# A graph attention edge loop in which VectorE adds the gathered rows to half of the scores

## The reference

```
s     = x_l[src] + x_r[dst] + e_attr @ W_e.T      # one row of 4 x 64 per edge
s     = leaky_relu(s, 0.2)
alpha = einsum('ehc,hc->eh', s, att)              # one score per edge and head
ex    = exp(alpha - segment_max(alpha, dst)[dst])
alpha = ex / (segment_sum(ex, dst)[dst] + 1e-16)
out   = segment_sum(alpha[..., None] * x_l[src], dst) + bias
```

## Time and profile before

| what | value |
|---|---|
| median of the runs | 3526.07 us |
| the profiled execution | 3518.4 us |
| its span | 3516.8 us |
| TensorE (PE) busy over the span | 3182.1 us, 90% |
| VectorE (DVE) | 1879.7 us, 53% |
| ScalarE (ACT) | 1363.2 us, 39% |
| GpSimd (POOL) | 1247.5 us, 35% |
| score products, line 1311, first and last start | 148.2 and 1376.5 us |

### The profile page before, as it was taken

The page is one execution under the profiler, slowest core; times in us unless marked ns, Lnnn a source line. Parts: engine busy times, 40 slices in busy tenths (PEclk is TensorE's granted clock), DMA queues, the critical chain, the costliest instruction groups (busy, mean ns, idle before and its releaser), DMA issues. The chain is left out here.

```text
span 3516.8 us, 52606 instructions
## 1 busy us (share of the span) xinstructions
PE 3182.1 (90%) x14467; PEld 2583.5 (73%) x14468; DVE 1879.7 (53%) x3767; ACT 1363.2 (39%) x4647; POOL 1247.5 (35%) x1195
## 2 busy tenths in 40 slices
PE   2799999999999999378998899799989896999998
PEld 1677777777777776266777677677867695888887
DVE  5677878777787787873436444633634330111102
ACT  0047677677777767431223113122312121222222
POOL 2376666666666663132103100300200043001016
PEclk9899999999999999588999999899989888999999
DMA  4576766766677665341111010000000143333323
GB/s 135 160 187 166 168 167 166 165 166 166 162 169 172 170 166 98 111 157 30 30 40 30 8 36 26 8 1 14 26 37 1 45 126 97 125 117 120 121 83 109
DMA packets 302415, 358.71 MB, mean 102 GB/s; under 512 B 164807, under 2 KB 223772, under 8 KB 298314
## 3 DMA queue, kind: packets, MB, share of 16 engines
q0 software_dynamic: 68240, 181.29, 19.9%
q1 hardware_dynamic: 233510, 173.64, 18.5%
q10 hardware_dynamic: 560, 2.35, 0.2%
HBM read 299.08 MB, written 57.01 MB: 101 GB/s over the span
## 5 line engine op out<-in xcount | busy, mean ns | idle before, releaser
L1311 PE MATMUL a_pS<-g_xr,a_lt 128*128 x1680 | 522.1, 393 | 26.1 <-DMA XS<-xl_d,a_ix 20.6
L1294 POOL DMA_INDIRECT a_g<-xl_d,a_ix x480 | 461.6, 962 | 220.9 <-PE a_pS L1312 133.2
L1405 ACT ACTIVATE b_m<-a_g,c_pcx 128x64 f32<-128x64 f32 x1856 | 454.6, 333 | 0.0
L1319 PE MATMUL b_pM<-b_m,b_oh 128*112 128x281 f32 x1680 | 443.6, 403 | 5.1 <-DVE g_acc L1447 3.5
L1440 DVE SCALAR_TENSOR_TENSOR a_r<-a_pS,g_attx 128x528 f32<-128x528 f32 x420 | 296.8, 707 | 242.5 <-PE a_pS L1312 233.6
L1294 POOL DMA_INDIRECT XS<-xl_d,a_ix x360 | 345.2, 959 | 134.9 <-issue 89.2
L113 POOL TENSOR_TENSOR m_rstd<-m_ve,m_mhalf 125x5 f32<-125x5 f32 x45 | 53.0, 1178 | 928.5 <-DVE m_ve L103 920.0
L1311 PEld LDWEIGHTS a_pS<-g_xr,a_lt 128*128 128x128 f32 x1680 | 310.6, 191 | 87.4 <-issue 30.0
L1319 PEld LDWEIGHTS b_pM<-b_m,b_oh 128*112 128x112 f32 x1680 | 291.0, 176 | 101.4 <-issue 10.7
L1994 ACT ACTIVATE f_hid<-f_pH,f_b 128x256 f32<-128x256 f32 (+2 forms) x360 | 169.2, 470 | 486.0 <-PE f_pH L1906 485.5
L421 PE MATMUL m_pH<-m_h,m_w 128*128 128x312 f32 (+1 forms) x1280 | 341.9, 428 | 7.7 <-DVE m_h L566 7.7
(11 more groups left out here) (348 smaller groups left out, 4444.7 us busy)
## 6 DMA issues: line engine op xcount, KB each, us to landing
a_db<-dl_d SPq DMA_DIRECT2D x212, 224.0 KB
f_w<-in_ffn_W1p SPq DMA_DIRECT2D x32, 1024.0 KB
m_w<-in_mix_W SPq DMA_DIRECT2D x8, 1024.0 KB
xg_d<-m_zero POOLq DMA_DIRECT2D x1, 8192.0 KB, 33.1
f_w<-in_ffn_W2p SPq DMA_DIRECT2D x8, 1024.0 KB
f_xg<-xg_d POOLq DMA_DIRECT2D x32, 256.0 KB, 3.7
y_d<-f_y POOLq DMA_DIRECT2D x32, 256.0 KB, 3.2
a_g<-xl_d,a_ix POOLq DMA_INDIRECT x480, 5.6
```

The source lines that it names most:

```text
L1294: p.indirect_dma_start(out=gathered(t)[:, j, :], out_offset=None, in_=xl_d, in_offset=bass.IndirectOffsetOnAxis(ap=IX[:, t // BSTEPS, n:n ...
L1311: pe.matmul(o, lt[:, j, :], XRW[:, bass.ds(ws[h], 1), :].rearrange("p a d -> p (a d)"), start=True, stop=False)
L1319: ins = pe.matmul(pM[0:WN, h, 0:MW], OH[:, b, j, :], M[:, b, j, :], start=(j == 2 * h), stop=(j == 2 * h + 1))
L1405: ins = a.activation(m[:, j, part], gathered(ts)[:, j, part], ACT.Copy, scale=of[:, first + j, h, 0:1])
```

## The change

`LIFTED` names five of the seven steps of a batch, tau 2 to 6. In these steps the identity product of the second pair is left out on TensorE. VectorE adds the gathered rows to the second pair instead (`lift`, from PSUM and SBUF into `a_r`), and gates that in place later, behind the one-hot for the sums (`lifted_gate`, from SBUF into SBUF). The semaphore that returns the PSUM banks to TensorE is renamed to `a_read0` and `a_read1`; for a lifted pair it is raised by the addition. The reduction of a lifted step also waits for the new gate (`a_gated`). The first pair, and both pairs of tau 0 and 1, are as they were.

```diff
--- before.py
+++ after.py
@@ -54,6 +54,7 @@
 WEIGH, SUM, ADD = 10, 11, 12
 AHEAD = 3
 SLOPE = 0.2
+LIFTED = (2, 3, 4, 5, 6)
 LOW = -float(2 ** 100)
 MH, MD = 8, 32
 FF = 1024
@@ -1305,11 +1306,13 @@
                         lt = LT[:, t % LTS, :, :]
 
                         def scores(h, ws):
-                            wait(pe, f"a_gated{h}", base, t)
+                            lifted = h == 1 and t % BSTEPS in LIFTED
+                            wait(pe, f"a_read{h}", base, t)
                             for j in (2 * h, 2 * h + 1):
                                 o = pS[0:TE, j, 0:GD]
-                                pe.matmul(o, lt[:, j, :], XRW[:, bass.ds(ws[h], 1), :].rearrange("p a d -> p (a d)"), start=True, stop=False)
-                                ins = pe.matmul(o, ident[:, :], gathered(t)[:, j, :], start=False, stop=True)
+                                ins = pe.matmul(o, lt[:, j, :], XRW[:, bass.ds(ws[h], 1), :].rearrange("p a d -> p (a d)"), start=True, stop=lifted)
+                                if not lifted:
+                                    ins = pe.matmul(o, ident[:, :], gathered(t)[:, j, :], start=False, stop=True)
                             ins.then_inc(s[f"a_scored{h}"], 1)
 
                         def sums(h):
@@ -1435,10 +1438,22 @@
                         par = 1 if odd else 0
                         scores = pA[0:CP, 0:TE]
 
+                        lifted = t % BSTEPS in LIFTED
+
+                        def lift():
+                            v.wait_ge(s[f"a_g{t}"], 64 * i + 64)
+                            wait(v, "a_scored1", base, t + 1)
+                            v.tensor_tensor(R[:, 2:4, :], pS[0:TE, 2:4, 0:GD], gathered(t)[:, 2:4, :], ALU.add).then_inc(s["a_read1"], 1)
+
                         def gate(h):
                             wait(v, f"a_scored{h}", base, t + 1)
                             v.scalar_tensor_tensor(out=R[:, 2 * h:2 * h + 2, :], in0=pS[0:TE, 2 * h:2 * h + 2, 0:GD], scalar=0.0,
-                                                   in1=attx[:, :].unsqueeze(1).broadcast_to([TE, 2, GD]), op0=ALU.max, op1=ALU.mult).then_inc(s[f"a_gated{h}"], 1)
+                                                   in1=attx[:, :].unsqueeze(1).broadcast_to([TE, 2, GD]), op0=ALU.max, op1=ALU.mult).then_inc(s[f"a_read{h}"], 1)
+
+                        def lifted_gate():
+                            wait(v, "a_read1", base, t + 1)
+                            v.scalar_tensor_tensor(out=R[:, 2:4, :], in0=R[:, 2:4, :], scalar=0.0,
+                                                   in1=attx[:, :].unsqueeze(1).broadcast_to([TE, 2, GD]), op0=ALU.max, op1=ALU.mult).then_inc(s["a_gated"], 1)
 
                         def add(h, at):
                             wait(v, f"b_summed{h}", base, t - ADD + 1)
@@ -1481,7 +1496,9 @@
                         elif tau == 3:
                             v.wait_ge(s["c_new"], n)
                             v.tensor_tensor(fade[:, :], by_item(ST[0:1, 1 - par, 0, 0:CP])[:, :, BI], pA[0:1, 0:GH], ALU.subtract).then_inc(s["c_step"], 1)
-                        if scoring:
+                        if scoring and lifted:
+                            lift()
+                        elif scoring:
                             gate(1)
                         if weighing and not scoring:
                             ts = (t - WEIGH) % RING
@@ -1495,6 +1512,8 @@
                             wait(v, "b_summed1", base, t - WEIGH - 1)
                             v.tensor_tensor(OH[:, t % 2, :, :], nodes[:, :].unsqueeze(1).broadcast_to([TE, IG, WN]),
                                             DLX[:, four(base, t - WEIGH)].unsqueeze(2).broadcast_to([TE, IG, WN]), ALU.is_equal).then_inc(s["b_onehot"], 1)
+                        if scoring and lifted:
+                            lifted_gate()
                         if tau == 1:
                             v.wait_ge(s["c_cols"], n)
                             v.tensor_copy(IN[:, :], pY[0:CP, 240:242]).then_inc(s["c_init"], 1)
@@ -1509,7 +1528,9 @@
                             v.wait_ge(s["c_step"], n)
                             v.tensor_scalar(fade[:, :], fade[:, :], 0.0, None, ALU.min).then_inc(s["c_less"], 1)
                         if scoring:
-                            wait(v, "a_gated1", base, t + 1)
+                            wait(v, "a_read1", base, t + 1)
+                            if lifted:
+                                v.wait_ge(s["a_gated"], 2 * len(LIFTED) * i + len([k for k in range(t + 1) if k % BSTEPS in LIFTED]))
                             i0 = IG * (t % BSTEPS)
                             v.tensor_reduce(AX_[:, t // BSTEPS, :, i0:i0 + IG].rearrange("p h i -> p i h"), R[:, :, :].rearrange("p i (h d) -> p i h d", h=GH),
                                             AX.X, ALU.add).then_inc(s["a_alpha"], 1)
```

## The result

The changed kernel takes 3496.14 us (median of 4 runs, 3494.87 to 3500.44), the kernel before beside it 3524.1 us. The ratio is 0.9923, 95% interval 0.9905 to 0.994: 28 us faster, where 90 were forecast and 3404 was the low and 3482 the high end. The profiled execution of the changed kernel took 3500.44 us, 18 less than that of before.

The account below looks back on a forecast made before the run. TensorE was taken to bound the edge loop at 41.09 us per batch; 4.45 saved less 1.3 of waiting for VectorE gains 3.15, times 28.6 batches 90 us: 3526 to 3436 us, range 3404 to 3482.

Parts of the forecast that it names:

- TensorE's saving: Edge loop: two identity products fewer per lifted step, 0.89 us, or 4.45 us per batch.
- VectorE's prices: Lifted steps: addition 0.692 us, SBUF gate 0.694, and a self-wait of 0.25; together 0.87 us more per step.
- 37.9 predicted: Edge loop's batch period in us: TensorE's 36.64 plus 1.3 of waiting, against 41.09 before.
- GpSimd's pace when nothing holds it: Edge loop: 1.274 us per gather, so 36.95 us per batch of 29, below the forecast period.
- the 1 us of cover per batch: Edge loop: what GpSimd has left per batch after the change, where before it had 4 us.
- Rival B: Edge loop: gathers become the bound through slipping landing or GpSimd pace; gain 60 to 31 us, 3466 to 3495; 17%.
- rival C: Lifted steps: the new SBUF gate waits for GpSimd's gathers, 0.95 us each; 45 us slower, 3571; 5%.
- a lead of three steps: Gathers ahead of TensorE: 15.6 us, less scores and issuing, so a landing of 8.7 us is still in time.
- TensorE's waits: For VectorE: 0.2 us before the sums of steps 5 and 6, 0.9 before step 0's transpose; 1.3 per batch.

Follow-up runs that it names:

- f1_onehot_first: Changed kernel with the one-hot for the sums moved ahead of the addition in lifted steps; 3448.32 us, ratio 0.9785 to the kernel before.
- f2_extra_gate: Kernel before plus one more VectorE gate in steps 2 to 6, both operands in SBUF, into a scratch buffer; 3524.2 us, ratio 1.0001.
- c2_reduce_for_gate: Changed kernel with the lifted steps' SBUF gate replaced by a reduction of the same columns, one SBUF operand; 3443.22 us, ratio 0.9767 to the kernel before.

## Why the prediction was wrong

**TensorE's saving and VectorE's prices were right.** The passes came at 0.697 and 0.700 for 0.692 and 0.694, and the quicker batches take 37.1 to 37.4 us. In f1_onehot_first, where the gathers are back at 0.962, the period is 38.39. That kernel has one self-wait more than the changed one; with the reduction in the gate's place, which has the changed kernel's order, it is 38.17, for 37.9 predicted. Of the 60 us between 3496 and 3436, these two kernels bring back 53 and 48.

**The step that failed** is "GpSimd's pace when nothing holds it is 17 gathers in 21.66 us, 1.274 each ... 36.95 us", taken over to the changed kernel. The gathers rose by 81.4 us in all. From the first to the last GpSimd now has 888.2 us of gathers, 30 staging gathers of 0.93 (27.9) and 870 gaps of 0.30 (261), 1177 of the 1338.9-142.4 = 1196.5 us: full to 98%, before 1095.7 of 1221.8, 90%. A batch is 29 x (1.057+0.30) = 39.4 us for GpSimd alone, more than TensorE's 36.64 and than my 37.9. GpSimd set the pace on average, and the 1 us of cover per batch that the prediction left it was gone. It shows in turns: in a batch of 37.2 us TensorE uses up GpSimd's lead, and in the next, behind the staging gathers, it waits. TensorE's waits for gathered rows between 300 and 1300 us, 37.3 + 5.7 us in 24.9 batches, are 1.7 us per batch, and 40.10-38.39 is 1.7.

**Rival B had the outcome, rival C the cause, and I had kept them apart.** B (17%) gave 31 to 60 us of gain for a slipping pace of GpSimd and named the DMA queue; the gain was 28. C (5%) saw that the gate's two SBUF operands could meet GpSimd, but only with VectorE as the one that waits; VectorE's gate kept its 0.70 us and GpSimd waited. The row on which I dismissed it, 210 one-hots at 615 to 620 ns, says nothing about the gathers beside them. Their maximum of 1233 and 1348 ns in the kernel before was the row to look at: the one-hot held gathers there too (the longest, 1.35 us, for one), but by the order in which the two engines ran only 16 of 840 met it. Of the two halves of the page's sentence that I weighed (the Trainium skill, SBUF — State Buffer, "Who interferes with whom"), the first holds here in its effect: two SBUF inputs contend with GpSimd. The second, which the page marks as inferred and by which descriptor generation is left alone, does not: 1.42 us instead of 0.95 beside one such pass, 1.88 beside two in a row.

**The late landing** of the gathers behind the staging, 8.4 us, is within the 8.7 that the prediction allowed for; but those 8.7 counted on a lead of three steps, and the lead was gone. With the gathers back at 0.962 TensorE's waits for them are all but gone (3.3 us in the same stretch), so I take the stall for a consequence of GpSimd's lost lead. Leaving the staging out was not tried.

**TensorE's waits** for the reduction and the additions exist (19.7 us before the transposes of the changed kernel, over 34 waits of TensorE and its weight load), but they did not set the time in it.

## What to carry to other kernels

Before adding work to one engine, look at the longest, not only the median, instruction of every engine that shares memory with it, and ask who is the one that waits. Where GpSimd issues indirect DMAs, every VectorE pass with two SBUF operands can hold one of them to its end, and passes back to back can add up: keep such passes few and apart. Here a pass with an operand in PSUM put between them was worth 48 us, for one more self-wait. An engine at 0.7 busy with a fixed gap between its instructions may be full: here each gather brings 0.30 us of gap, and 0.76 busy was 98% occupied.

## What the runs showed of the hardware

- GpSimd's gather instruction (0.95 us) ended 0.82 us behind the end of a VectorE pass with two SBUF operands that was under way 0.12 us after its start: 1.42 us beside one gate (f2_extra_gate), 1.88 us beside an unbroken 1.23 us of two passes (changed kernel); VectorE's passes were not longer. The longest of the changed kernel took 2.26 us, beside three in a row. The one-hot for the scores (line 1433, one tensor and a column from SBUF) held gathers too, up to 1.23 us.
- Beside VectorE passes of the same 528 columns with one operand in PSUM and one in SBUF the gathers kept 0.947 us (209 of them in the changed kernel), and beside the reduction from SBUF in c2_reduce_for_gate as well (82 of them).
- After 4.74 us of idleness TensorE came back at the lower of its two clock levels, 1.2 instead of 2.4 GHz (granted clock 0.61 from 724.00 to 728.40): 724.90-723.97 = 0.93 us for a product instead of 0.445, and 728.43-723.97 = 4.46 us for scores that else take 2.67. The granted clock of the whole window was 0.97.
- Chips differ: the kernel before took 3524 to 3526 us in three measurements and 3690 and 3710 us on two other chips, where waits in the edge loop end by "remote" events and a change could have the other sign (the reduction in the gate's place: ratio 0.9767 on one chip, 1.0089 on another).
